# Two conditioned linear layers: the first tile of w1 issued by another engine

## The chip, the cores and the metric

The kernel runs on one core of one Trainium2 chip. The metric is device time in microseconds (us), the median of several runs. One further execution was taken with the hardware profiler; its rows are what the text reads.

## The reference

Two layers are applied one after the other to x of shape (8, 256, 1024), each with a residual, a dense 1024x1024 weight and a low-rank correction that an index selects per batch row:

```
def _L0_cond_ref(x, labeler_index, W, lora_A, lora_B_w):
    base = einsum('bsi,oi->bso', x, W)
    low = einsum('bsi,bir->bsr', x, lora_A[labeler_index])
    return base + einsum('bsr,or->bso', low, lora_B_w) * (16 / 32)

def _L1_cond_ref(x, adapter_mapping, W, b, lora_As, lora_Bs):
    base_out = einsum('bti,oi->bto', x, W) + b
    lora_h = einsum('bti,bir->btr', x, lora_As[adapter_mapping])
    return base_out + einsum('btr,bro->bto', lora_h, lora_Bs[adapter_mapping]) * (32 / 16)

x = x + _L0_cond_ref(x, index0, W0, A0, B0w)      # index0 in 0..2, rank 32
x = x + _L1_cond_ref(x, index1, W1, b, A1s, B1s)  # index1 in 0..23, rank 16
```

Everything is float32.

## The kernel before

The kernel first multiplies the two weights together, each with the identity added to its diagonal (the residuals), so that the batch loop needs one dense product. That product V and the products of the batch loop are made by a seven-product scheme on halves of the matrices. Each float32 operand is split into a high part (rounded to fp32r) and a low part (the rest), and a product is three matmuls: high by high, high by low, low by high.

A weight is cut into four quarters of 512x512, and a quarter into four tiles of 128 partitions by 512 columns, 256 KB each. Tiles of w0 are called `a` (a11, a12, a21, a22), and each of their 128 rows is 2 KB without a gap. Tiles of w1 are called `n` (n11, n12, n21, n22) and come in runs of 128 numbers, 512 bytes. They arrive untransposed: TensorE transposes each `n` tile into a PSUM bank by four 128x128 transposes (line 1228), which gives `b`. The first of the seven products is A11 by B11, and it is what the core does first.

What stands around the change, engine by engine:

- SyncE (line 264 on) issues every load of the kernel. Its loop at line 274 issues, for j = 0 to 3, first the tile n11[j] (`load_n`, recorded as L272), then a11[j] (`load_a`, L269); each has its own semaphore. All later weight tiles follow in the same queue.
- VectorE (lines 749 to 764) waits for the identity (`eye`, made by GpSimd at the start) and for n11[0], adds the identity to its diagonal block (L718), then waits for a11[0]: it casts the right half of it to a11_hi, adds the identity, casts the left half (L753), and then makes b11_lo[0] and a11_lo[0].
- GpSimd adds the identity to the later tiles.
- ScalarE (line 491 on) has b11_hi[0] as its first work: a copy out of the bank that holds the transposed tile, after `turned` says that the transposes are done. Its activation table is loaded once, ahead of that.
- TensorE (line 1308 on) starts with 14 matmuls on constants (`warm_up`, 256 columns each, bf16), then runs `turn_b11(0)`, which waits for n11[0] and does the four transposes, the block with the identity last; then five more warm-up matmuls; then `vm1_high(0)`, the first eight real matmuls, which wait for b11_hi[0] and for the halves of a11_hi[0]; then `turn_b11(1)` and so on.

Every step from n11[0] to `vm1_high(0)` is therefore a chain: load, transposes, ScalarE's copy, first real matmul. TensorE's list of instructions is fixed; no planner reorders it.

Of the kernel before, what the change touches and what calls it, by code (L numbers as in the profile page):

```python
# [12 lines left out]
P = 128  # L13
# [7 lines left out]
def two_layer_lora_kernel(nc, x, label0, slot1, w0, a0, b0w, w1, bias, a1, b1, out):  # L21
    B, S, D = x.shape
    NL, _, R0 = a0.shape
    NS, _, R1 = a1.shape
    KT = D // P
    CH = S
# [21 lines left out]
    def at(name, shape, dt, offset):  # L48
        size = 4
        for n in shape[1:]:  # L50
            size *= n
        assert base + offset + size <= nc.sbuf_usable_end, name
        return nc.alloc_sbuf_tensor_at(name, shape, dt, offset=base + offset)
# [12 lines left out]
    n11 = at("n11", [P, HK, HK, P], F32, 12 * SLOT)  # L66
# [85 lines left out]
    with ExitStack() as ctx:  # L152
        bank = [ctx.enter_context(nc.psum_tensor(f"bank{n}", [P, 512], F32)) for n in range(8)]

        def sem(name):
            return ctx.enter_context(nc.semaphore(name))
# [3 lines left out]
        n11_in = [sem(f"n11_in{j}") for j in range(HK)]  # L160
# [91 lines left out]
        def quarter(t, g):  # L252
            return t[:, HK * (g % 2):HK * (g % 2) + HK, P * (g // 2):P * (g // 2) + P]

        def last_half(h):
            dst = out[B - 1, :, sides[h]].rearrange("(p odd) i -> odd p i", odd=2)
            return dst[0], y[:, C11, sides[h]]
# [5 lines left out]
        @block.sync  # L263
        def _(sp):
            w0_v = w0.rearrange("(b j p) (a i) -> p b j a i", b=2, p=P, a=2)
            w1_v = w1.rearrange("(n t p) (b j k) -> p n t b j k", n=2, p=P, b=2, k=P)

            def load_a(tile, a, b, j, there):
                sp.dma_start(tile[:, j, :], w0_v[:, b, j, a, :]).then_inc(there, 16)  # L269

            def load_n(tile, n, b, j, there):
                sp.dma_start(tile[:, j, :, :], w1_v[:, n, :, b, j, :]).then_inc(there, 16)  # L272

            for j in range(HK):
                load_n(n11, 0, 0, j, n11_in[j])
                load_a(a11, 0, 0, j, a11_in[j])
                if j == 2:
                    sp.dma_start(index[0:1, 0:B], label0.rearrange("(o b) -> o b", o=1)).then_inc(index_in, 16)
                    sp.dma_start(index[0:1, B:2 * B], slot1.rearrange("(o b) -> o b", o=1)).then_inc(index_in, 16)
# [85 lines left out]
            for h in range(2):  # L365
                sp.wait_ge(half_made, h + 1)
                sp.dma_start(*last_half(h)).then_inc(y_out[C11], 16)
# [98 lines left out]
        def _(act):  # L466
# [6 lines left out]
            def bank_copy(tile, m, ps, made):  # L473
                copy(tile[:, m, :], ps[:, :], made)
# [8 lines left out]
            def b11_high(j):  # L483
                act.wait_ge(turned, j + 1)
                bank_copy(b11_hi, j, TURN_BANK[j], w1_hi_made)

            def b11_copy(j):
                act.wait_ge(w1_lo_made, j + 1)
                bank_copy(b11, j, TURN_BANK[j], w1_made)

            for j in range(2):
                b11_high(j)
                b11_copy(j)
# [1105 lines left out]
```

## Time and profile before

| what | value |
|---|---|
| median of 3 runs | 294.64 us (294.39 to 294.78) |
| the profiled execution's own time | 294.97 us |
| its span in the profile | 293.2 us |
| mean granted TensorE clock | 0.999 |
| TensorE matmul busy | 289.5 us, 99% of the span |
| VectorE, ScalarE, GpSimd busy | 83%, 52%, 11% |

PE is TensorE's matmul, PEld its weight load (each matmul has one, which runs beside the matmul before), DVE VectorE, ACT ScalarE, POOL GpSimd, and SPq the queue in which SyncE issues its transfers. The ends of matmuls are modelled in this profile, so a short pause of PE is better read from the weight loads than from PE's busy time.

### The profile page before, as it was taken

Reading aid. Unit: us, or ns where it says so; the run is one execution under the profiler, and the core shown is the slowest. Engines: PE = TensorE matmul, PEld = TensorE weight load, DVE = VectorE, ACT = ScalarE, POOL = GpSimd, SP = SyncE. Lnnn points to the kernel's source line nnn. Section 1 sums busy time; section 2 is a strip of 40 time slices with the busy share of each in tenths; the row PEclk is TensorE's granted clock in tenths of the full one; section 3 lists DMA queues with packets and bytes.
Section 4 is the critical chain, followed back from the end, with each engine's and each line's share of the span. In section 5 each row is a group of like instructions: output and inputs, shape, how many; then the busy total and the mean of one; then the engine's idle time right before and its main releaser. Section 6 shows DMA issues by size and latency. Waiting matters only on the chain.

```text
span 293.2 us, 4450 instructions
## 1 busy us (share of the span) xinstructions
PE 289.5 (99%) x1337; PEld 236.1 (81%) x1337; DVE 242.9 (83%) x368; ACT 153.6 (52%) x270; POOL 31.3 (11%) x81
## 2 busy tenths in 40 slices
PE   8999999999999999999999999999999999999996
PEld 6888888888888888878878878878878878878875
DVE  3779998999999999999996897797798698695432
ACT  3574677879257637464453463373364355355120
POOL 0716500010000501000100100100100100100000
PEclk9999999999999999999999999999999999999999
DMA  6999530800006610074277077068068059013004
GB/s 200 315 275 345 79 43 6 141 1 2 0 0 110 97 28 1 6 125 157 46 117 199 22 120 198 18 101 221 6 108 212 15 101 233 6 36 144 0 1 145
DMA packets 100803, 29.17 MB, mean 99 GB/s; under 512 B 85548, under 2 KB 93996, under 8 KB 100788
## 3 DMA queue, kind: packets, MB, share of 16 engines
q1 hardware_dynamic: 100788, 28.99, 42.4%
q8 instruction: 7, 0.11, 0.2%
q14 instruction: 8, 0.07, 0.1%
HBM read 20.59 MB, written 8.39 MB: 99 GB/s over the span
## 4 chain that ended last, share of the span: by engine, by line
PE 99%; DVE 0%; issue 0%
PE bank L1204 95%; PE bank L1228 3%; PE bank L1449 1%; PE bank L1416 0%; DVE y L718 0%
## 5 line engine op out<-in xcount | busy, mean ns | idle before, releaser
L1204 PE MATMUL bank<-v_hi,lhs 128*128 128x512 f32 (+1 forms) x136 | 42.6, 378 | 0.0
L1204 PE MATMUL bank<-vt_lo,s_hi 128*128 128x512 f32 x96 | 37.4, 389 | 0.0
L1204 PE MATMUL bank<-vt_hi,s_hi 128*128 128x512 f32 x96 | 37.4, 389 | 0.0
L1204 PE MATMUL bank<-vt_hi,s_lo 128*128 128x512 f32 x96 | 37.4, 389 | 0.0
L969 DVE STREAM_TRANSPOSE xt<-raw 128x512 int32<-128x512 int32 x32 | 32.5, 1076 | 0.5 <-DMA raw<-in_x 0.4
L1204 PEld LDWEIGHTS bank<-v_hi,lhs 128*128 128x128 f32 x136 | 25.1, 188 | 4.8
L468 ACT ACTIVATE lhs<-xt 128x512 fp32r<-128x512 f32 x32 | 19.6, 626 | 13.0 <-PE bank L1204 12.7
L1204 PE MATMUL bank<-v_lo,lhs 128*128 128x512 f32 (+1 forms) x68 | 25.9, 380 | 0.0
L1204 PE MATMUL bank<-vt_hi,lhs 128*128 128x512 f32 x64 | 22.1, 406 | 0.0
L718 DVE TENSOR_TENSOR lhs<-xt,lhs 128x512 fp32r<-128x512 f32 x32 | 21.7, 687 | 0.3
L434 POOL CAST ac<-c_hi 128x128 fp32r (+1 forms) x16 | 7.1, 446 | 135.7 <-PE bank L1204 98.6
L718 DVE TENSOR_TENSOR s_lo<-s_sum,s_hi 128x512 fp32r<-128x512 f32 x32 | 21.2, 686 | 0.2 <-ACT s_hi L468 0.2
L1204 PEld LDWEIGHTS bank<-vt_lo,s_hi 128*128 128x128 f32 x96 | 18.0, 188 | 3.7
L1204 PEld LDWEIGHTS bank<-vt_hi,s_hi 128*128 128x128 f32 x96 | 18.0, 188 | 3.7
L1204 PEld LDWEIGHTS bank<-vt_hi,s_lo 128*128 128x128 f32 x96 | 18.0, 188 | 3.7
L468 ACT ACTIVATE s_hi<-s_sum 128x512 fp32r<-128x512 f32 x32 | 19.1, 624 | 2.1 <-DVE s_sum L718 1.8
L1204 PE MATMUL bank<-t_hi,s_hi 128*128 128x512 f32 x48 | 19.1, 397 | 0.0
L1204 PE MATMUL bank<-t_hi,s_lo 128*128 128x512 f32 x48 | 18.8, 391 | 0.0
L1204 PE MATMUL bank<-t_lo,s_hi 128*128 128x512 f32 x48 | 18.7, 390 | 0.0
L468 ACT ACTIVATE u_part<-bank 64x256 f32<-64x256 f32 x8 | 3.1, 381 | 28.0 <-PE bank L1204 28.0
L718 DVE TENSOR_TENSOR y<-bank,u_sum 128x512 f32<-128x512 f32 x16 | 11.0, 687 | 6.6 <-PE bank L1204 6.6
L468 ACT ACTIVATE vt_hi<-vt 128x512 fp32r<-128x512 f32 x16 | 10.1, 631 | 11.0 <-DVE vt L718 10.5
(167 smaller groups left out, 665.1 us busy)
## 6 DMA issues: line engine op xcount, KB each, us to landing
raw<-in_x SPq DMA_DIRECT2D x32, 256.0 KB, 4.8
out<-y SPq DMA_DIRECT2D x31, 256.0 KB, 2.7
n<-in_L_cond_W SPq DMA_DIRECT2D x16, 256.0 KB, 5.6
a<-in_L_cond_W SPq DMA_DIRECT2D x16, 256.0 KB, 5.6
a_raw<-in_L_cond_lora_A SPq DMA_DIRECT2D x8, 128.0 KB, 2.4
b_raw<-in_L_cond_lora_Bs SPq DMA_DIRECT2D x16, 64.0 KB, 2.2
e_raw<-in_L_cond_lora_Bs SPq DMA_DIRECT2D x32, 32.0 KB, 1.8
a_raw<-in_L_cond_lora_As SPq DMA_DIRECT2D x8, 64.0 KB, 2.6
```

The costliest lines, as they stand in the source:

```text
L434: nc.gpsimd.tensor_copy(ac[:, :, at_col:at_col + R1], c_hi[:, :, cols].bitcast(F32)).then_inc(ac_c_made, 1)
L468: nc.scalar.activation(out_ap, in_ap, COPY, scale=scale).then_inc(made, 1)
L718: nc.vector.tensor_tensor(out_ap, one, other, op).then_inc(made, 1)
L969: nc.vector.transpose(xt[:, n, :, :].rearrange("p e (s sb) -> p sb e s", sb=GR).bitcast(I32), rows[:, n // 2, n % 2].bitcast(I32)).then_in ...
L1204: return nc.tensor.matmul(ps, lhsT, rhs, start=start, stop=stop, skip_group_check=more)
L1228: last = nc.tensor.transpose(ps[:, P * t:P * t + P], tile[:, j, t, :], eye[:, :])
L1449: return nc.tensor.matmul(ps, e_st[rows, P * t:P * t + P], e_p[rows, cols], start=False, stop=True, skip_group_check=True, tile_position=( ...
```

## The change

The first tile of w1, n11[0], is issued by ScalarE ahead of its first copy, instead of by SyncE at the head of its queue. SyncE's loop leaves it out, so its first transfer is a11[0], and all other loads keep their order. The semaphore, the source and the destination of the transfer stay the same. The view `w1_v` moves out of SyncE's block so that both can use it.

```diff
@@ -252,6 +252,8 @@
+        w1_v = w1.rearrange("(n t p) (b j k) -> p n t b j k", n=2, p=P, b=2, k=P)
+
@@ -263,7 +265,6 @@
         @block.sync
         def _(sp):
             w0_v = w0.rearrange("(b j p) (a i) -> p b j a i", b=2, p=P, a=2)
-            w1_v = w1.rearrange("(n t p) (b j k) -> p n t b j k", n=2, p=P, b=2, k=P)
@@ -272,7 +273,9 @@
             for j in range(HK):
-                load_n(n11, 0, 0, j, n11_in[j])
+
+                if j > 0:
+                    load_n(n11, 0, 0, j, n11_in[j])
                 load_a(a11, 0, 0, j, a11_in[j])
@@ -488,6 +491,7 @@
+            act.dma_start(n11[:, 0, :, :], w1_v[:, 0, :, 0, 0, :]).then_inc(n11_in[0], 16)
             for j in range(2):
                 b11_high(j)
                 b11_copy(j)
```

## Rows read from the trace of the kernel before

**Rows 1.** The page: TensorE's busy time, and the chain by engine.

```profile
PE 289.5 (99%) x1337; PEld 236.1 (81%) x1337; DVE 242.9 (83%) x368; ACT 153.6 (52%) x270; POOL 31.3 (11%) x81
...
PE 99%; DVE 0%; issue 0%
```

**Rows 2.** The chain that ended last, in order of time: start, us, what.

```profile
0.83 3.15 PE bank L1204 x14
3.97 0.03 issue
4.00 1.09 PE bank L1228 x4
...
8.04 0.44 PE bank L1228 x4
...
241.80 22.21 PE bank L1204 x97
```

**Rows 3.** PE's busy time in three long stretches.

```profile
core 0: us, PE busy (x), PEclk, DMA share, GB/s
9.16:46.00 36.84, 36.84 (x193) 1.00 0.75 193
46.00:128.00 82.00, 82.00 (x372) 1.00 0.24 41
128.00:290.40 162.40, 162.38 (x740) 1.00 0.43 101
```

**Rows 4.** Timeline of the first 9 us: start, duration, engine, line, tiles, [idle before].

```profile
0.78 0.45 SPq L272 DMA_DIRECT2D n<-in_L_cond_W  x1
0.79 1.28 ACT L468 ACT_TABLE_LOAD   x1 [0.79 <-PEq L1588]
...
1.29 0.49 SPq L269 DMA_DIRECT2D a<-in_L_cond_W  x1
1.83 0.43 SPq L272 DMA_DIRECT2D n<-in_L_cond_W  x1
...
3.97 0.29 DVE L718 TENSOR_TENSOR n<-n,eye 128x128 f32<-128x128 f32 x1 [3.97 <-DMA n<-in_L_cond_W]
3.98 0.71 PEld L1228 LDWEIGHTS bank<-eye,n 128*128 128x128 f32 x4 [0.48 <-issue]
...
5.07 0.29 DVE L753 CAST a_hi<-a 128x256 fp32r<-128x256 f32 x1 [0.81 <-DMA a<-in_L_cond_W]
5.13 0.60 ACT L468 ACTIVATE b_hi<-bank 128x512 fp32r<-128x512 f32 x1 [3.06 <-PE bank L1228]
...
5.78 0.93 PEld L1204 LDWEIGHTS bank<-b_hi,a_hi 128*128 128x128 f32 x4
...
7.32 0.46 POOL L376 TENSOR_TENSOR n<-n,eye 128x128 f32<-128x128 f32 x1 [5.81 <-DMA n<-in_L_cond_W]
7.65 0.58 PEld L1228 LDWEIGHTS bank<-eye,n 128*128 128x128 f32 x4
...
9.16 0.76 PEld L1204 LDWEIGHTS bank<-b_hi,a_hi 128*128 128x128 f32 x4 [0.19 <-ACT b_hi L468]
```

**Rows 5.** Tile `n`, all its loads: from issue to landing.

```profile
DMA to landing us min/median/max: 3.1/5.6/8.0
```

**Rows 6.** Busy time, DMA share and bandwidth in stretches of half a microsecond.

```profile
1.50:2.00 0.50, 0.50 (x4) 0.37 (x3) 0.00 (x0) 0.50 (x1) 0.01 (x1) 1.00 0.07 20
2.00:2.50 0.50, 0.50 (x5) 0.32 (x3) 0.00 (x0) 0.07 (x1) 0.00 (x0) 1.00 0.61 181
2.50:3.00 0.50, 0.50 (x4) 0.38 (x3) 0.00 (x0) 0.00 (x0) 0.00 (x0) 1.00 1.07 332
3.00:3.50 0.50, 0.50 (x4) 0.37 (x3) 0.00 (x0) 0.00 (x0) 0.00 (x0) 1.00 1.33 369
```

## The prediction

> **What bounds the kernel now.** I read the page first. TensorE is busy for 289.5 of 293.2 us, and the chain that ended last is TensorE for 99% [rows 1]. An engine that is as full as that sets the time, and all that can move the end is its idle time or the duration of its instructions. So the next question is where in its fixed list TensorE pauses. The chain in order of time [rows 2] gives the head: 14 warm-up matmuls from 0.83 us, then the first transposes at 4.00. The long stretches [rows 3] say that nothing is left later: 36.84 of 36.84 us, 82.00 of 82.00, and 162.38 of 162.40 us are busy. Nothing behind 9.16 us has slack that could absorb a delay at the head, and nothing there waits for a load that could come sooner. A shift of the first matmuls shifts the end by as much.
>
> The timeline of the head [rows 4] shows what TensorE's first work waits for. n11[0] is issued at 0.78; VectorE's addition and TensorE's first transposing weight load start within 0.01 us of each other, at 3.97 and 3.98, and the latter has 0.48 us of idle time before it. That is the landing of n11[0], 3.1 us behind its issue [rows 5]. From there the chain has no slack: transposes from 3.98 on, ScalarE's copy at 5.13 for 0.60 us, which ends at 5.73, and the first real weight load at 5.78. The other inputs of that first matmul are earlier: the first cast of a11[0] begins at 5.07 and takes 0.29, so it ends at 5.36, 0.42 us ahead. The five extra warm-up matmuls only fill the time between. Behind this there is one more pause, 0.19 us ahead of the weight load at 9.16, and it waits for a copy of ScalarE, whose transposes began at 7.65 right after TensorE's own earlier work and not when a load came.
>
> So one load decides, n11[0], and its price is plain: a landing later by d moves the end by about d; a landing sooner by d can give at most the 0.48 us of idle time.
>
> **The change part by part.** Durations are from the profiled execution, so the sum is made against its own time of 294.97 us (span 293.2, 1.8 around it, which I leave unchanged); the median of the runs is 294.64, 0.33 below, and the same difference is carried over to it.
>
> *SyncE's queue.* It loses one issue, from 0.78 to the next at 1.29, so 0.51 us [rows 4]. a11[0] is issued at 0.78 instead of 1.29, n11[1] at about 1.32 instead of 1.83, and each later load 0.51 us sooner until its queue waits for something else. What is this worth? a11[0] had 0.42 us of slack already, n11[1] is taken by GpSimd at 7.32 and by TensorE's transposes only at 7.65, when TensorE is through with what stands before it. After 9.16 nothing waits. So I cost all of these at nothing: TensorE's own work hides them. If that cover went, they would be a gain, bounded by the 0.19 us pause at 9.16.
>
> *ScalarE's list.* It gains one issue, of the kind that took SyncE 0.45 us. It issues once, ahead of a copy before which ScalarE is idle for 3.06 us [rows 4]. The table load (1.28 us from 0.79) would then run from about 1.24 to 2.52, and the copy is not before 5.13. Nothing is queued behind it that anyone needs earlier. Cost 0, hidden by that idle time, as long as the issue comes ahead of the table load (the other order is a rival below).
>
> *The landing of n11[0].* Its issue stays where it was, near 0.79. What is new is what moves beside it. Before, it had the DMA engines to itself for its first half microsecond of issue, and a11[0] came behind it in the same queue. Now a11[0] is issued at the same time in another queue, and n11[1] 0.5 us later. The rows of bandwidth [rows 6] show what this means: traffic begins at about 2.0, is 181 GB/s up to 2.5 and 332 and 369 GB/s in the next two half microseconds, with the engines' share at 1.07 and 1.33. They are full from 2.5 us on, which is just while n11[0] is moved. Two loads of 256 KB that share full engines cannot both keep their time. Bounds: if all of a11[0] goes in before the end of n11[0], it is late by 262144 bytes at 332 to 369 GB/s, 0.71 to 0.79 us. If the engines take turns by pieces, and n11's pieces (512 bytes) are a quarter of a11's (2 KB), then a11[0] is through when n11[0] has a quarter done, and the other three quarters share turns with the same pieces of n11[1]: 0.75 for a11[0] and three quarters of 0.75 for n11[1], 1.3 us. At the other end, if descriptors of n11[0] keep ahead of those of a11[0] as one queue has them now, the delay is 0; below nothing I see only this: the first packets could start no earlier, since the issue is no earlier, so a gain needs a landing that is less spread over the 16 engines, and is bounded by the idle 0.48 us. I take 0.75 us, the price of one load in front, which lies between the two ways of sharing and is nearest to what the bandwidth rows give without further assumption.
>
> The Trainium skill speaks against the change here. In "DMA: Bandwidth & Descriptors", section "Issuing engines are not separate DMA queues", it says that transfers of SyncE, ScalarE and GpSimd all run on the same 16 DMA engines and interleave, and that a second issuing engine only saves issue time, which is usually small. By that rule nothing is gained for n11[0], whose issue is not earlier, and the delay by sharing stands. Section "Queues, rings and completion order" says that each engine goes round between the queues packet by packet; that is the interleaving of which I priced both ends. The rows of before show one queue only and can't say which it is.
>
> *What the shifted head saves.* The four transposes in the first tile take 1.09 us and those of the second 0.44 [rows 2], and the 14 warm-up matmuls of 256 columns take 3.15 us, 0.225 us each, 1.14 columns per ns. In the batch loop 97 matmuls, nearly all of 512 columns, take 22.21 us [rows 2], 0.229 each, 2.2 columns per ns. The granted clock reads 1.00 in all rows, yet the head plainly runs at the 1.2 GHz level and the rest at 2.4. The rise lies between the transposes at 4.00 and those at 8.04. The first four real weight loads take 0.93 us from 5.78 (0.23 each), so all but one or two matmuls are behind the rise already. A later start therefore saves at most 0.05 to 0.1 us here; I take 0.05. The same limits a gain: matmuls that start sooner would run at 1.2 GHz, twice as long, so 0.48 us sooner gives back only about half, 0.25.
>
> *Sum.* 0.75 - 0.05 + 0 + 0 = +0.70 us: 295.67 for an execution like the profiled one, 295.34 against the median. I forecast 295.3 us, +0.24%.
>
> **The rivals.**
>
> 1. *Not slower: n11[0] keeps its place.* Condition: the queue that is served first moves n11[0] as before, because a11[0]'s rows are behind it on the engines, or because the transfer's duration is mostly the fixed way there and back. For it speaks that of the 3.1 us to landing [rows 5] the 256 KB at 332 GB/s make only 0.8, and that the share before 2.5 us is 0.61, not full. Against it speaks the 1.07 and 1.33 right after. Price 0 to 0.2 us; time 294.65. It decides if n11[0] lands before 4.2.
>
> 2. *The table load goes first.* Condition: ScalarE runs its 1.28 us table load, which starts at 0.79, ahead of the issue. Then n11[0] is issued at 2.07, 1.28 late, and behind a11[0] and n11[1], so 0.75 more, less 0.05: +2.0 us, 296.6. For it speaks that the table load is the first thing that ScalarE does now. Against it: it carries the line of the copies, so it belongs to the first copy, and the new issue stands ahead of that. The Trainium skill, "ScalarE: Activation LUTs", section "What happens when an `exp` ACTIVATE runs", puts the load right before the ACTIVATE that needs it; the trace has its start 4.3 us ahead of the copy, which agrees only if the wait belongs to the copy.
>
> 3. *The clock rises later.* Condition: TensorE's pause ahead of the transposes grows from 0.48 to 1.2 us, and the 2.4 GHz level comes later than the first real matmuls. Each matmul of 512 columns then costs 0.43 instead of 0.23 us; with 8 of them (`vm1_high(0)`) 1.6 us on top of the 0.70: 296.9. For it: the rise before came after a stretch that was busy but for 0.48 us. Against it: the five warm-up matmuls stay between.
>
> 4. *A gain.* The landing is sooner, or the pause at 9.16 goes: at most 0.25 + 0.19 = 0.44 us, 294.2. For it only the emptier SyncE queue; no step needs it.
>
> **How the numbers follow.** Forecast 0.55, with a delay between 0.3 and 1.35 us, so 294.9 to 296.0; rival 1 0.20; rival 2 0.12; rival 3 0.08; rival 4 0.05. About 0.2% (0.59 us, 295.23 and above) is what a measurement of this kernel tells from no change. Of the forecast's 0.55, 0.40 lies beyond that and 0.15 within. Slower: 0.40 + 0.12 + 0.08 = 0.60. Same: 0.15 + 0.20 + most of rival 4, 0.02 = 0.37. Faster: 0.03. The range goes from 294.5 to 296.6: it takes in rival 1 and the lower part of rival 2, and leaves out most of rival 3, the upper half of rival 2 and the gains, 0.17 together.
>
> **What would show it.** In the timeline after: ScalarE's row of the issue at 0.79 and its table load behind it (rival 2 if the order is turned). The first transposing weight load should start at about 4.7 instead of 3.98, with about 1.2 us of idle time before it, and the first real weight load at 6.5 instead of 5.78; these two shifts should equal the shift of the span. SyncE's issues should all stand 0.51 us sooner, a11[0] should land before n11[0], and the stretches from 9.9 us on should be full as before. Wrong is the forecast if the first transposes start before 4.2 (rival 1), or if the transposes of the second tile take more than 0.5 us (rival 3), or if a new pause shows behind 10 us.

## The result

The changed kernel takes 297.27 us (median of 8, 295.65 to 297.43) against 294.96 for the kernel before in the same comparison (294.39 to 295.89). The ratio is 1.0069 with a 95% interval of 1.0058 to 1.0081, so the change costs about 2.0 us (the medians differ by 2.3). The direction was forecast, the size was not: 295.3 was predicted, and the time lies above the range's upper end of 296.6.

The profiled execution took 296.80 us with a span of 295.0, against 294.97 and 293.2 before. The page of the changed kernel, the lines that answer to [rows 1]:

```profile
PE 290.1 (98%) x1337; PEld 236.3 (80%) x1337; DVE 242.7 (82%) x368; ACT 153.5 (52%) x270; POOL 28.8 (10%) x81
...
PE 97%; DMA 1%; DVE 0%; issue 0%
```

The chain has a piece that was not in it before: 1% of it is a transfer. The chain of the changed kernel in order of time, its first 14 us (start, us, what):

```profile
0.79 4.37 DMA n<-in_L_cond_W
5.15 0.14 issue
5.29 1.08 PE bank L1232 x4
6.37 3.50 PE bank L1208 x13
9.87 0.44 PE bank L1232 x4
10.30 2.81 PE bank L1208 x12
```

The same view of the kernel before, the rows that [rows 2] leaves out (lines are 4 lower there):

```profile
5.09 2.95 PE bank L1204 x13
...
8.47 2.79 PE bank L1204 x12
```

These rows hold the whole loss of the profiled execution. The first transposes start at 5.29 instead of 4.00, 1.29 us later, because the load ends at 5.15. The 13 matmuls after them (five for warm-up, eight real ones) take 3.50 instead of 2.95 us, 0.55 more. The transposes of the second tile therefore start at 9.87 instead of 8.04, 1.83 us later; from there on the pieces are as long as before (2.81 and 2.79), and the profiled times differ by 296.80 - 294.97 = 1.83. Nothing is given back later. PE's busy time in the three long stretches, shifted by about 2 us against [rows 3]:

```profile
11.00:48.00 37.00, 37.00 (x193) 31.28 (x192) 34.26 (x44) 22.82 (x35) 10.01 (x18) 1.00 0.70 174
48.00:130.00 82.00, 82.00 (x370) 67.70 (x369) 78.85 (x114) 52.75 (x89) 7.12 (x16) 1.00 0.24 41
130.00:292.20 162.20, 162.20 (x739) 130.91 (x738) 126.18 (x202) 74.90 (x143) 8.11 (x36) 1.00 0.43 101
```

The timeline of the head of the changed kernel, which answers to [rows 4]:

```profile
0.78 0.40 SPq L270 DMA_DIRECT2D a<-in_L_cond_W  x1
0.79 0.47 ACTq L494 DMA_DIRECT2D n<-in_L_cond_W  x1
...
1.23 0.42 SPq L273 DMA_DIRECT2D n<-in_L_cond_W  x1
1.29 1.28 ACT L471 ACT_TABLE_LOAD   x1 [1.29 <-PEq L1592]
...
5.25 0.71 PEld L1232 LDWEIGHTS bank<-eye,n 128*128 128x128 f32 x4 [1.76 <-issue]
...
7.06 1.37 PEld L1208 LDWEIGHTS bank<-b_hi,a_hi 128*128 128x128 f32 x4
```

The last row shows the second term: four weight loads take 1.37 us where they took 0.93, and their starts come to lie 0.43 us apart, the 1.2 GHz level, up to the first of the next four at 8.52; those four run at 0.23. So the first four of the eight real matmuls were at the lower level. Before, all but the first two starts were 0.23 apart. The granted clock of a window reads 1.00 in both heads, so durations have to be read.

Why did n11[0] come so late, with its issue still at 0.79? The DMA view of the changed kernel by queue (q1 is SyncE's, q10 ScalarE's: packets, MB, share of 16 engines), first for 1.5 to 2.8 us, then for 2.8 to 3.5:

```profile
q1 hardware_dynamic: 103, 0.20, 60.2%
```

```profile
q10 hardware_dynamic: 211, 0.11, 54.1%
q1 hardware_dynamic: 38, 0.06, 39.0%
```

Up to 2.8 us the engines moved only SyncE's queue, and not a single packet of n11[0]. Nothing moves before 1.8 us, so the 60% of this stretch are 78% of the 1.0 us since the first packet, against the 1.07 and 1.33 of [rows 6]. In that time 103 of the 128 rows of a11[0] went. This is not two loads sharing full engines. ScalarE's queue moved nothing for a microsecond after SyncE's had begun, and only then did the two share.

### The profile page after: what moved, and what is told of

Read it like the earlier page. It is cut to its first block, busy times and chain, and to the rows that moved or that the text cites. A ratio compares the mean times of both kernels' runs of the same rounds, so it can differ in the third digit from the quotient of the medians.

```text
span 295.0 us, 4450 instructions
## 1 busy us (share of the span) xinstructions
PE 290.1 (98%) x1337; PEld 236.3 (80%) x1337; DVE 242.7 (82%) x368; ACT 153.5 (52%) x270; POOL 28.8 (10%) x81
## 4 chain that ended last, share of the span: by engine, by line
PE 97%; DMA 1%; DVE 0%; issue 0%
PE bank L1208 93%; PE bank L1232 3%; DMA n<-in_L_cond_W 1%; PE bank L1453 1%; PE bank L1420 0%; DVE y L722 0%
## 5 line engine op out<-in xcount | busy, mean ns | idle before, releaser
L1208 PE MATMUL bank<-lhs,ac 128*128 128x512 f32 x64 | 15.8, 389 | 0.0
```

Of the source, the lines that this page charges most:

```text
L1208: return nc.tensor.matmul(ps, lhsT, rhs, start=start, stop=stop, skip_group_check=more)
```

## Experiments

Each was timed beside the kernel before (295.0 to 295.1 us in these comparisons).

**One queue alone.** Is a transfer from ScalarE slow by itself? SyncE issues nothing until n11[0] is there.

```diff
@@ changed kernel, SyncE
+            sp.wait_ge(n11_in[0], 16)
             for j in range(HK):
```

> ScalarE issues n11[0] at 0.79 us and SyncE issues nothing until it has landed. Theory A (one source of descriptors serves the issues of both queues in turn, and a11[0] was served first): with nothing ahead, n11[0] lands 3.1 us after its issue as it did from SyncE's queue, near 3.9. Theory B (a transfer from ScalarE's queue starts about 1 us later whatever else runs): first bytes near 2.8 and landing near 4.8 to 5.1, as in the changed kernel. Theory C (sharing of full DMA engines): near 3.9 as A; the next run tells A from C. The execution as a whole is slower, since a11[0] and all other loads come 3 us late: 297 to 300 us.

Measured 296.81 us in one execution. The tile view of `n` up to 2 us, from issue to landing, first for this run, then for the changed kernel (in which it holds n11[0] and n11[1]):

```profile
DMA to landing us min/median/max: 3.0/3.0/3.0
```

```profile
DMA to landing us min/median/max: 4.4/4.5/4.7
```

3.0 us from ScalarE's queue is as fast as 3.1 from SyncE's [rows 5]. Theory B is out: the late landing comes from what runs beside it. The time came out just below the expected 297 to 300.

**Who goes first.** SyncE's first issue waits for the memset of the identity.

```diff
@@ changed kernel, SyncE
+            sp.wait_ge(eye_steps, 1)
             for j in range(HK):
```

> The changed kernel, but SyncE's first issue waits for the memset of the identity, which ends near 1.0 us, so ScalarE's issue at 0.79 is the first. Theory A: n11[0] is served first and lands near 3.9 as before, a11[0] behind it near 5.0; time as before, 294.6 to 295.3. Theory B: n11[0] still lands near 5; time 296.5 to 297.5. Theory C: a11[0] still shares the engines with it, landing near 4.5, time about 295.5.

Measured 296.99 us (296.44 to 297.43), ratio 1.0065 (1.0049 to 1.0081). Timeline of this run:

```profile
0.79 0.43 ACTq L495 DMA_DIRECT2D n<-in_L_cond_W  x1
...
1.02 0.40 SPq L270 DMA_DIRECT2D a<-in_L_cond_W  x1
...
4.67 0.29 DVE L723 TENSOR_TENSOR n<-n,eye 128x128 f32<-128x128 f32 x1 [4.67 <-DMA n<-in_L_cond_W]
4.67 0.71 PEld L1233 LDWEIGHTS bank<-eye,n 128*128 128x128 f32 x4 [1.18 <-issue]
```

A miss for A and C alike; the time is in B's range, but its landing near 5 did not come, and the run before had ruled B out. n11[0] was now first, and TensorE's start on it came at 4.67, earlier than 5.25 but 0.7 us later than 3.98. So there are two parts in the delay: about 0.6 for being served second and about 0.7 from the other queue's load close behind it. The second part is not a sharing of the engines alone either. The DMA view of 1.5 to 2.8 us, this run and then the kernel before:

```profile
q10 hardware_dynamic: 200, 0.10, 27.8%
```

```profile
q1 hardware_dynamic: 378, 0.19, 49.6%
```

SyncE's queue had moved nothing yet, the engines were at 28%, and still n11[0] had only 200 of its 512 packets through instead of 378. And although 0.6 us of the delay was gone, the time stayed that of the changed kernel, which pointed at a second cause.

**A larger head start.** SyncE waits for the identity to be complete, 1.53 us.

```diff
@@ changed kernel, SyncE
+            sp.wait_ge(eye_steps, 2)
```

> The changed kernel with SyncE's first issue behind the whole making of the identity, near 1.5 us instead of 1.0. With SyncE at 1.0 n11[0] began first and still landed at 4.6, 0.7 us later than in one queue. If that is sharing with a11[0]'s bytes, a later a11[0] gives less of it: landing 4.0 to 4.3, time 295.3 to 296.3. If it is a fixed cost of two queues, landing stays at 4.6 and the time at 296.9.

Measured 295.22 us (294.63 to 295.79), ratio 1.0001 (0.9992 to 1.0011): the whole loss is gone. Timeline:

```profile
1.53 0.40 SPq L270 DMA_DIRECT2D a<-in_L_cond_W  x1
...
3.98 0.72 PEld L1233 LDWEIGHTS bank<-eye,n 128*128 128x128 f32 x4 [0.49 <-issue]
```

n11[0] is from ScalarE's queue here too, and the transposes start at 3.98 as before the change. Two queues are no fixed cost; a second load 0.23 us behind the first was one, a load 0.74 us behind it was not. What it saves at the head it does not turn into a gain: a11[0] is first cast at 5.76, and in this execution (295.79 us, the slowest of the ten) the first real weight load starts at 6.17, 0.39 us later than before the change.

**The swap.** n11[0] stays with SyncE, a11[0] is issued by ScalarE.

```diff
@@ kernel before, SyncE and ScalarE
-                load_a(a11, 0, 0, j, a11_in[j])
+                if j > 0:
+                    load_a(a11, 0, 0, j, a11_in[j])
...
+            act.dma_start(a11[:, 0, :], w0_v[:, 0, 0, 0, :]).then_inc(a11_in[0], 16)
```

> n11[0] stays at the head of SyncE's queue and a11[0] is issued by ScalarE at 0.79. Theory A: the queue whose issue arrives first is served first; SyncE's was first by 0.004 us, so n11[0] lands near 3.9 and a11[0] near 5.0, and the time is that of the kernel before within 0.1%, 294.7 to 295.3. Theory B: a11[0] lands near 5 as well, so no difference from A in the time. Theory C: n11[0] lands 0.5 to 1 us later than 3.9, and the time is 295.5 to 296.

Measured 296.87 us (295.66 to 297.43), ratio 1.0051 (1.0038 to 1.0065). None of the three theories had this right. Timeline:

```profile
0.78 1.01 SPq L273 DMA_DIRECT2D n<-in_L_cond_W  x2
0.79 0.42 ACTq L493 DMA_DIRECT2D a<-in_L_cond_W  x1
...
5.17 0.71 PEld L1231 LDWEIGHTS bank<-eye,n 128*128 128x128 f32 x4 [1.68 <-issue]
```

And the DMA view of 1.5 to 2.8 us holds one queue only, this time ScalarE's:

```profile
q10 hardware_dynamic: 71, 0.15, 48.9%
```

So it is no preference for an engine: issued together, a11[0] went first from either queue, and n11[0] waited. What decides is open. a11[0] has 2 KB rows, and its issue is also the shorter one (0.40 and 0.42 us against 0.47 and 0.46), so it ends first. The next run was to tell these apart.

**Two tiles of the same shape.** SyncE's first transfer is n11[1] instead of a11[0].

```diff
@@ changed kernel, SyncE
+                if j == 0:
+                    load_n(n11, 0, 0, 1, n11_in[1])
-                if j > 0:
+                if j > 1:
                     load_n(n11, 0, 0, j, n11_in[j])
                 load_a(a11, 0, 0, j, a11_in[j])
```

> The changed kernel, but SyncE's first transfer is n11[1] (512-byte runs, its issue takes as long as that of n11[0]) and a11[0] follows. In the changed kernel and in the swap the tile with 2 KB rows was served first, whichever queue it was in; its issue was also the first to end (1.18 against 1.25, 1.20 against 1.24). Theory A1 (the issue that ends first is served first): SyncE's n11[1] ends at about 1.23, ScalarE's n11[0] at 1.25, so n11[1] goes first and n11[0] begins near 2.7 and lands at 4.8 to 5.3; time 296.9 to 297.5. Theory A2 (with equal shapes neither waits for the other, or ScalarE's goes first): n11[0] begins at 1.9 and lands at 3.9 to 4.6; time 295 to 296.9, and a11[0] is late by one tile.

Measured 296.67 us (295.29 to 296.98), ratio 1.0040 (1.0024 to 1.0057). Timeline:

```profile
4.74 0.72 PEld L1234 LDWEIGHTS bank<-eye,n 128*128 128x128 f32 x4 [1.26 <-issue]
...
6.75 0.29 DVE L759 CAST a_hi<-a 128x256 fp32r<-128x256 f32 x1 [1.72 <-DMA a<-in_L_cond_W]
```

The transposes began at 4.74, and up to 2.3 us SyncE's queue alone had moved packets, 138 of them; n11[0] began 0.4 us behind it instead of 1.0. That is between A1 and A2: the issue that ends first went first, as A1 says, but the other waited less than its numbers. Inconclusive. The time says nothing of it: the first real weight load, at 7.16, here waited for a11[0], which was now the late tile and first cast at 6.75. What stands is that n11[0] is late beside any other load issued at its side.

**Halves in both queues.**

```diff
@@ kernel before
-                load_n(n11, 0, 0, j, n11_in[j])
+                if j == 0:
+                    sp.dma_start(n11[:, 0, 0:2, :], w1_v[:, 0, 0:2, 0, 0, :]).then_inc(n11_in[0], 16)
+                else:
+                    load_n(n11, 0, 0, j, n11_in[j])
...
+            act.dma_start(n11[:, 0, 2:4, :], w1_v[:, 0, 2:4, 0, 0, :]).then_inc(n11_in[0], 16)
```

(n11_in[0] is awaited at 32.)

> n11[0] in two halves of 128 KB, the first issued by SyncE and the second by ScalarE, both at 0.78; the rest of the queue as before, a11[0] behind SyncE's half. Theory A (descriptors of the two queues come from one source, one transfer after the other): no gain from the second queue, the later half begins about half a microsecond after the first, and then has a11[0] beside it; landing 4.2 to 4.6, time 295.4 to 296.5. Rival (each queue has its own source): both halves start at 1.9, landing 3.4 to 3.7, time 294.6 to 295.0.

Measured 294.99 us (294.81 to 295.62), ratio 1.0003 (0.9994 to 1.0013). The DMA view up to 2.5 us, and a row of the timeline:

```profile
q1 hardware_dynamic: 92, 0.05, 18.2%
```

```profile
5.94 0.77 PEld L1209 LDWEIGHTS bank<-b_hi,a_hi 128*128 128x128 f32 x4 [0.21 <-ACT b_hi L472]
```

ScalarE's half had moved nothing by 2.5 us, the transposes began at 4.13. Two queues moved the one tile no faster than one. The landing, 0.15 us later than before, was in neither forecast's range, the time in the rival's. In the profiled execution the 0.15 us were given back by the clock: the first four real weight loads are at the 2.4 GHz level from the start (0.77 us instead of 0.93), and the transposes of the second tile begin at 7.66, against 7.65 before.

**The idle time made short.** The changed kernel with enough warm-up matmuls to reach the landing.

```diff
@@ changed kernel, TensorE
-            warm_up(14)
+            warm_up(21)
```

> The changed kernel with 21 warm-up matmuls instead of 14, so that TensorE is busy up to 5.05 us while n11[0] lands at 5.15. If the idle time of 1.76 us kept the clock low (theory: 0.6 of the loss is late clock), the transposes of the first tile or at least the first real matmuls run at the 2.4 GHz level, and the time is 0.6 to 1.1 us below the changed kernel: 296.2 to 296.7. If the clock's rise has nothing to do with it, the time stays at 297.3.

Measured 295.71 us (295.53 to 296.20), ratio 1.0023 (1.0010 to 1.0035): the seven matmuls, which compute nothing that is used, give back about 1.4 of the 2.0 us, more than the 0.6 to 1.1 expected. Timeline:

```profile
5.21 0.48 PEld L1232 LDWEIGHTS bank<-eye,n 128*128 128x128 f32 x4 [0.51 <-issue]
...
6.56 0.76 PEld L1208 LDWEIGHTS bank<-b_hi,a_hi 128*128 128x128 f32 x4 [0.41 <-ACT b_hi L471]
```

The landing is as late as in the changed kernel, but TensorE had only 0.51 us of idle time instead of 1.76. The four transposes took 0.48 instead of 0.71 us of weight loads and the real ones 0.76 instead of 1.37: both at the 2.4 GHz level. The swap with 21 warm-up matmuls is the same test on another kernel.

> The swap (a11[0] from ScalarE, n11[0] from SyncE) with 21 warm-up matmuls. n11[0] lands at 5.1 as in the swap. If the two terms, late landing and late clock, are separate and the second is due to the idle time, this is as the changed kernel with 21: 295.5 to 296.0, 1.2 us below the swap.

Measured 295.70 us (295.58 to 296.25), ratio 1.0032 (1.0022 to 1.0041). The median is 1.2 us below the swap's, as expected; the ratios, 1.0032 against 1.0051, say 0.6, since three of the swap's eleven executions were already as quick. The transposes start at 5.23, and the first real weight loads take 0.77: a late landing without a late clock. The two terms can be had one without the other.

**The idle time made long, with no load moved.** The kernel before with fewer warm-up matmuls.

```diff
@@ kernel before, TensorE
-            warm_up(14)
+            warm_up(8)
```

> The kernel before with 8 warm-up matmuls ahead of the transposes instead of 14: n11[0] lands at 3.9 as before, but TensorE is idle from about 2.3 to 4.0 us, 1.7 us as in the changed kernel. If that idle time by itself makes the clock rise late, the time goes up by 0.5 to 1.3 us, to 295.6 to 296.4, with no load moved, and the real matmuls at 5.8 run at the 1.2 GHz level. If only the landing matters: 295.1, no change.

Measured 296.80 us (296.61 to 297.06), ratio 1.0061 (1.0046 to 1.0077). Chain of this run in order of time:

```profile
0.78 3.00 DMA n<-in_L_cond_W
3.78 0.14 issue
3.92 1.08 PE bank L1228 x4
5.00 4.38 PE bank L1204 x13
9.38 0.44 PE bank L1228 x4
```

And from its timeline:

```profile
3.89 0.71 PEld L1228 LDWEIGHTS bank<-eye,n 128*128 128x128 f32 x4 [1.68 <-issue]
...
5.69 1.37 PEld L1204 LDWEIGHTS bank<-b_hi,a_hi 128*128 128x128 f32 x4
```

The load lands at 3.78 and the transposes start at 3.92, both slightly earlier than before, and yet 1.8 us are lost, more than the 0.5 to 1.3 expected. The 13 matmuls take 4.38 us instead of 2.95. An idle time of 1.68 us ahead of the transposes, about that of the changed kernel, goes with a TensorE that stays at 1.2 GHz through the eight real matmuls. Fewer warm-up matmuls mean both a longer pause and less work ahead of it, and no run separates the two here; between the changed kernel and the one before, with 14 each, it is the pause that grew. Of the timed 1.8 us the profiled span shows 1.4 (294.6 against 293.2); the rest isn't placed.

The same with 11 warm-up matmuls, idle for 1.06 us:

> The kernel before with 11 warm-up matmuls: n11[0] lands at 3.9, idle time ahead of the transposes about 1.1 us, between the 0.43 of before (295.0 us) and the 1.7 of the version with 8 (296.8). If the loss grows with the idle time, or falls on a part of the executions, the median is between, 295.4 to 296.4; if it comes all at once, it is at one of the two ends. It tells how much idle time this head of the kernel bears.

Measured 296.07 us, ratio 1.0029 (1.0013 to 1.0046), but spread over 294.8 to 296.68, where the kernel before spans 1.2 us. Between the two ends lies no fixed smaller loss, but executions with and without it: four at 294.8 to 295.4 and six at 296.0 to 296.7. In the profiled one, a lucky one at 295.26, the clock had risen ahead of the first real matmuls; none of the six was profiled.

```profile
3.92 0.71 PEld L1228 LDWEIGHTS bank<-eye,n 128*128 128x128 f32 x4 [1.06 <-issue]
...
4.60 0.54 PEld L1204 LDWEIGHTS bank<-const-bfloat16-1.0 128*128 128x128 bf16 x5
```

And with 16, which leave no idle time:

> The kernel before with 16 warm-up matmuls, which fill the 0.43 us that TensorE is idle ahead of the transposes. n11[0] lands at 3.9 as before. If the idle time delays the clock's rise in some executions: 0.3 to 0.8 us less than before, 294.3 to 294.8, and a narrower spread. If not: 295.1 as before.

Measured 295.09 us (294.82 to 295.50), ratio 1.0007 (0.9998 to 1.0016). Nothing is won by filling the 0.48 us of idle time. In the profiled execution two things cancel: the warm-up matmuls reach past the landing, so that ScalarE's copy starts at 5.29 instead of 5.13, and the first four real weight loads take 0.75 us instead of 0.93; the transposes of the second tile begin at 7.66, as before (7.65). No version tried beats the kernel before.

## Why the prediction was wrong

**Right.** One load decides; its landing passes 1:1 to the first real matmul (the transposes 1.29 us later, the real weight loads 7.06 - 5.78 = 1.28); nothing behind absorbs or adds; ScalarE's issue and table load are hidden, in the order assumed (0.79, then 1.29), so rival 2 is out; the earlier loads of SyncE are worth nothing: a11[0] is issued at 0.78, n11[1] at 1.23 and a11[1] at 1.71, and no wait that set the end went away. Rival 4's bound on a gain was never tested, since no run landed n11[0] clearly sooner.

**The landing was mis-sized.** The step "if all of a11[0] goes in before the end of n11[0]" gave 0.75 us by sharing bandwidth. Measured was 1.28, near the upper bound of 1.3, but by another mechanism than the one that the bound was worked out from. n11[0] moved no packet until 2.8 us while the engines were at 78% on average, not full; it was held back first and shared later, and the run with ScalarE's issue ahead shows both parts at about 0.6 and 0.7. The row of [rows 5] and the bandwidth in [rows 6] were from one queue; they could not show how two queues issued at one time are served. The Trainium skill ("DMA: Bandwidth & Descriptors", "Issuing engines are not separate DMA queues") says that a second engine saves only the time of the issue, and no run here contradicts that; it also says that the transfers interleave with each other, and from 1.8 to 2.8 us they did not, here or in the swap.

**The second term failed outright.** "A later start therefore saves at most 0.05 to 0.1 us" took the moment of the clock's rise as fixed. It is not: the later landing lengthened TensorE's idle time to 1.76 us, and with it the rise moved behind the first four of the eight real matmuls. In the profiled execution this term was +0.55 us (3.50 - 2.95) where the sum had -0.05. I had this as rival 3, at 0.08, with the argument that five warm-up matmuls stay between; they did not help. Its time, 296.9, is the nearest of all to the 297.27 measured, though the sign that I gave for it, transposes of the second tile above 0.5 us, did not show (0.44): the clock had risen before them, at about 8.5. Its price of 1.6 us on top of the landing was close to the timed one: 21 warm-up matmuls take 1.4 us off the changed kernel, and 8 instead of 14 put 1.8 on the kernel before. So the 2.0 us are about 0.7 for the late landing at an early clock (the changed kernel with 21, ratio 1.0023; the swap with 21 has 1.0032, 0.9 us) and about 1.4 for the late clock. The profiled execution of the changed kernel splits otherwise, 1.28 and 0.55, because the kernel before has its transposes at the lower level too, and the profiled execution was one of the quicker ones.

**The chances.** Landing and clock were set as alternatives, one case each. They are one after the other: the first causes the second. A forecast that takes an idle time from 0.48 to 1.2 us ahead of work that the clock decides has to carry the clock's price in its main case.

**Still open:** why a11[0] is served first from either queue (row size or end of issue), and why the waiting was 0.4 us behind a tile of 512-byte runs and 1.0 behind one of 2 KB rows. That the descriptors of both queues come from one source (theory A) would fit packets that are held back while the engines are not full, but no run shows that source, and in the form in which A was put down it missed three times, with SyncE behind by 0.23 us, in the swap and in the time of the halves. Open too is which executions get the early clock: each kernel has one trace, and it shows one of them.

## What to carry to other kernels

When a load feeds the first work of a full engine, leave nothing beside it in another queue when it starts (0.23 us behind it was too close here, 0.74 was not); a second issuing engine does not make it sooner, and a transfer issued in the same moment can go ahead of it, here for 1.0 us and four fifths of its 256 KB. When such a load gets later, count TensorE's idle time before and after, and price the first real matmuls at the lower clock as soon as that idle time grows past what was harmless. Warm-up matmuls should reach to within half a microsecond of the landing: when it moved out by 1.3 us, seven more were worth 1.4 us here.

## What the runs showed of the hardware

- Two transfers of 256 KB issued within 0.01 us of each other from two queues: the first packets of one come 1.0 us behind those of the other (1.8 and 2.8 us), with the DMA engines at 78% in between (64% in the swap). With 0.23 us of head start the order follows the issue but the landing is still 0.7 us late; with 0.74 us it is as in one queue, 3.1 us from its issue.
- TensorE idle ahead of the transposes, with the load's landing unchanged: none (295.09 us), 0.48 (295.0), 1.06 (294.8 to 296.7), 1.68 (296.80). A pause of half a microsecond cost no time on balance, one of 1.7 cost 1.8 us. The Trainium skill ("TensorE: Matmul & The Clock Gate", "Part 1: The HAM clock gate") says that the number of matmuls at the lower clock varies from run to run of one kernel; the spread of the times at 1.06 us is in line with that, though the matmuls were counted in one execution only.
- The eleven executions of the swap show the same two kinds: three at 295.7 and eight at 296.8 to 297.4.
